# First attention: group outputs taken inside the next Q/K normalisation; local layers: first K and Q at the end of the FFN

## The chip, the cores and the metric

The kernel runs on one core of a Trainium2 chip. The metric is the time of one execution on the device in microseconds (us), the median of several. The core has a matrix engine (TensorE, PE in the profile; PEld is its weight load), three others that compute (VectorE = DVE, ScalarE = ACT, GpSimd = POOL) and SyncE (SP), which here issues all DMAs. Each engine runs its own program in order; they wait for each other at semaphores.

## The reference, cut to what matters

`x` has 8 batches of 512 rows of 128 values, all in float32. Two blocks are added to it in turn:

```python
xn = layernorm(x)
x = x + attn0(xn) + ffn0(xn)   # attn0: differential causal attention, 16 q/k heads of 8, 8 value heads of 16
                               #   q, k: rms-normalised, rotated; y = y1 - lambda * y2, then Wproj
                               # ffn0: one linear layer on inputs quantised in blocks of 32
xn = layernorm(x)
x = x + attn1(xn) + local(xn)  # attn1: plain attention, 16 heads of 8
def local(x):                  # 6 layers, 16 heads of 64, window 32
    for i in range(6):
        x = attn_layer(shift_tokens(x), ...) + x
        x = ffn_layer(shift_tokens(x), ...) + x
```

`shift_tokens` takes the upper half of the columns from the row before. `attn_layer` forms q, k, v with one weight of 128 x 3072, l2-normalises and rotates q and k, attends within windows of 32 rows and the window before, and multiplies by Wo. `ffn_layer` is a layer norm, a gated product and a product back to 128 columns.

## The kernel before, in words

The program has four phases, one behind another with a barrier between: the first attention with its linear layer (up to about 400 us), the second attention (to about 895 us), the six local layers (to about 4403 us), and the sum and the output.

**First attention.** All engines walk through one list `steps` of triples (b, j, k): batch b, group j of four heads (four groups to a batch), head k. Group number t = 4b + j. In step (b, j, k) TensorE makes the scores of head k of group t and, from k = 1 on, the products with the values of group t - 1; ScalarE takes the exponentials. At k = 0 ScalarE copies the sums of group t - 2 to `OT` (L448), at k = 1 TensorE transposes them (L369) and VectorE divides them into `Y` (`outputs`, L520 to L528). The other work is laid between these steps and shares one PSUM bank (7), which each user may take only after the reader of the last user is done (`claim`):
- `in_prep(b)`, batches -2 to 5: batch b + 2 is prepared. Transposes of its normalised rows `XL` (L363) at (0, 0), Q/K/V products (L377) at (0, 2), (0, 3), (1, 0), (1, 2), VectorE's copies of them (L630, L631), ScalarE's squares (L490) and VectorE's `normal` (L508 to L513) at (1, 3): a reduction, eleven short operations of which ten are the root (`rsqrt`, L111 to L115), and a multiplication in place (L513). Then GpSimd rotates queries and keys (`rotated`, L695 to L698, twice), TensorE transposes them at (3, 0) and (3, 2) (L424), VectorE copies them to `QR` and `KR` (L648), GpSimd splits them into three bfloat16 parts (`parts`, L706 and L709), and SyncE writes these to DRAM and packs the groups from there. For batch 1 the transposes stand at (0, 0, 0) and (0, 0, 1).
- `done(b)`, batches 1 to 8: the outputs of batch b - 1. Transposes of `Y` (L396) at (1, 3), of the quantised rows `xd` (L402) at (2, 0), the projection (L412, L413) at (2, 3); VectorE adds the bias (`pr`, L636) and adds the result to the rows `X1` (L639).
- VectorE's quantising of batch b is a generator of 17 operations (`quant_steps`, L195 to L211), of which it runs one at the end of each step of the batch (`next(work)`) and the rest at (3, 3).
- Before step (0, 0, 0) VectorE runs the rest of its list `early`, which ends with the normalisation of the rows of batches 2 to 7 (`scaled(2, B)`, L571) and the quantising of the weight.

**Local layers.** Each engine has a loop over the six layers. A layer's attention goes over 32 row tiles of 128 (`tiles`), three tiles in flight: in a slot the front tile gets K, V, Q products (L1383, L1393 or L1454, L1448; the first tile has its own order, 1), ScalarE squares and copies them, VectorE multiplies by cosines and sines (L1667, L1672) and sums the squares, GpSimd takes the root and scales (L1286 to L1308); the middle tile is transposed (L1424, L1467), the last one attends. SyncE copies the values into windows, 20 DMAs a tile. The FFN (`layer`, run through `ahead`) takes the batches in pairs; at its end TensorE transposes the rows of batch 0 (`rows_up`, L1331) for the next layer. ScalarE copies them to `xsT` (L1524, L1525) at the head of its next turn of the layer loop, and TensorE's first K product stands at the head of its own next turn, behind the waits for these rows and for the weights. The weights of layer l's attention are loaded by SyncE at the head of its turn l, once the attention of layer l - 1 is done.

## Time and profile before

| | us |
|---|---|
| median of 3 runs (lowest, highest) | 4410.02 (4403.59, 4414.05) |
| the profiled execution: its time | 4421.74 |
| its span, first to last instruction | 4419.9 |
| TensorE busy | 4084.9 (92%) |
| VectorE busy | 3323.8 (75%) |
| GpSimd busy | 2596.7 (59%) |
| ScalarE busy | 2372.8 (54%) |

The mean granted TensorE clock was 0.976 of full speed. A row of the view in order of time has: start, duration, engine, line, operation, output and inputs, how many instructions are merged into it, and in brackets the engine's idle time before it and what ended it. VectorE's next instruction can start some 0.08 us before the end shown for the last.

### The profile page before, as it was taken

The numbers are of one execution on the slowest core, as the hardware profiler recorded it, in microseconds if no ns is written. First come the engines' busy times: TensorE is split into PE (matmuls) and PEld (weight loads), VectorE is DVE, ScalarE is ACT, GpSimd is POOL, SyncE is SP. The second block draws the span as 40 slices with busy tenths as digits, with TensorE's granted clock in tenths as the row PEclk, the third lists the DMA queues.
The fourth block names the chain that finished last, engine by engine and source line by source line (L and its number), as shares of the span: only waits on it lengthen the run. The fifth ranks groups of instructions, "written<-read, shape, count | busy, mean of one in ns | idle before, by whom it ended". The sixth has DMA issues, their size and how long they took to land. (4 is left out here: it accounts for less than half of the span.)

```text
span 4419.9 us, 164515 instructions
## 1 busy us (share of the span) xinstructions
PE 4084.9 (92%) x68421; PEld 2658.5 (60%) x68421; DVE 3323.8 (75%) x5603; ACT 2372.8 (54%) x3396; POOL 2596.7 (59%) x3647
## 2 busy tenths in 40 slices
PE   4888999979998899988999989999899998899997
PEld 2554333357676576765777666777557676577765
DVE  7785988768876678776787767878668886688775
ACT  3654777745554455544555544555445554455543
POOL 5452111077774477762878727777357875377770
PEclk9998999989999999999999999999999999999999
DMA  2222111033332133221332303323123232133320
GB/s 76 86 79 65 54 56 53 28 87 81 79 80 56 48 80 80 75 61 46 78 82 76 78 25 82 84 73 83 42 58 83 77 81 64 38 79 79 81 68 20
DMA packets 216797, 298.60 MB, mean 68 GB/s; under 512 B 44241, under 2 KB 110801, under 8 KB 215377
## 3 DMA queue, kind: packets, MB, share of 16 engines
q1 hardware_dynamic: 216144, 288.46, 24.3%
q8 instruction: 585, 9.58, 0.9%
q14 instruction: 68, 0.55, 0.0%
HBM read 58.13 MB, written 14.68 MB: 16 GB/s over the span
## 5 line engine op out<-in xcount | busy, mean ns | idle before, releaser
L1542 ACT ACTIVATE ls_r<-PS 128x1024 f32<-128x1024 f32 x192 | 196.6, 1024 | 782.8 <-PE PS L1383 782.8
L1677 DVE TENSOR_REDUCE ls_ss<-ls_r 128x16 f32<-128x1024 f32 x384 | 465.7, 1214 | 99.1 <-ACT ls_r L1579 99.1
L1667 DVE TENSOR_TENSOR ls_a<-PS,TC 128x1024 f32<-128x1024 f32 x384 | 467.5, 1219 | 94.1 <-ACT ls_r L1542 90.8
L1286 POOL TENSOR_TENSOR ls_a<-ls_a,ls_q 128x1024 f32<-128x1024 f32 x192 | 453.9, 2364 | 99.0 <-DVE ls_q L1672 99.0
L1672 DVE TENSOR_TENSOR ls_q<-PS,TS 128x512 f32<-128x512 f32 x768 | 491.3, 681 | 0.0
L1306 POOL TENSOR_TENSOR ls_a<-ls_a,ls_q 128x1024 f32<-128x1024 f32 x192 | 456.7, 2379 | 0.0
L1448 PE MATMUL PS<-WQ,ls_xsT 128*128 128x512 f32 x768 | 398.8, 642 | 4.0 <-issue 4.0
L1579 ACT ACTIVATE ls_r<-PS 128x1024 f32<-128x1024 f32 x186 | 190.7, 1026 | 392.7 <-PE PS L1448 392.7
L1474 PE MATMUL PS<-WO,ls_r 128*128 128x128 f32 x3072 | 398.6, 284 | 0.5 <-ACT ls_r L1583 0.5
L1383 PE MATMUL PS<-WQ,ls_xsT 128*128 128x512 f32 x768 | 382.5, 621 | 16.3 <-issue 9.9
L1308 POOL TENSOR_TENSOR ls_a<-ls_a,ls_rn 128x1024 f32<-128x1024 f32 x192 | 365.6, 1904 | 15.1
L1303 POOL TENSOR_TENSOR ls_a<-ls_a,ls_rn 128x1024 f32<-128x1024 f32 x192 | 365.4, 1903 | 15.0
L1474 PEld LDWEIGHTS PS<-WO,ls_r 128*128 128x128 f32 x3072 | 363.2, 194 | 18.1 <-ACT ls_r L1583 1.9
L1393 PE MATMUL PS<-WQ,ls_xsT 128*128 128x512 f32 x744 | 349.6, 592 | 0.0
L1019 DVE TENSOR_REDUCE mxs<-PS 128x2 f32<-128x1024 f32 x256 | 305.9, 1220 | 50.9 <-PE PS L873 48.6
L954 ACT ACTIVATE PT<-PS 128x512 f32<-128x512 f32 x512 | 282.0, 599 | 109.0 <-PE PS L882 102.8
L1704 DVE RECIPROCAL ls_rc<-PS 128x14 f32<-128x14 f32 x192 | 47.2, 246 | 372.3 <-PE PS L1438 372.2
L1317 POOL TENSOR_TENSOR ls_r<-XL,B 128x512 f32<-128x512 f32 x48 | 61.1, 1294 | 452.5 <-DVE XL L1751 326.3
L1438 PE MATMUL PS<-ls_vb,ls_q 64*32 64x65 f32 x24576 | 289.6, 228 | 40.0 <-issue 29.8
L1368 PE MATMUL PS<-ls_kT,ls_qT 64*32 64x64 f32 x24576 | 317.4, 225 | 0.0
L1684 DVE TENSOR_REDUCE ls_mx<-PS 128x8 f32<-128x512 f32 x384 | 263.3, 686 | 70.8 <-PE PS L1368 66.6
L1368 PEld LDWEIGHTS PS<-ls_kT,ls_qT 64*32 64x32 f32 x24576 | 279.8, 105 | 50.0 <-issue 43.5
(274 smaller groups left out, 8653.9 us busy)
## 6 DMA issues: line engine op xcount, KB each, us to landing
ls_vb<-ls_vt SPq DMA_DIRECT2D x1152, 130.0 KB
ls_vb<-ls_vt SPq DMA_DIRECT2D x672, 65.0 KB
QT<-scratch SPq DMA_DIRECT2D x576, 32.0 KB
KT<-scratch SPq DMA_DIRECT2D x576, 32.0 KB
ls_xs<-XL SPq DMA_DIRECT2D x42, 256.0 KB, 3.3
WQ<-wqkv SPq DMA_DIRECT2D x6, 1536.0 KB, 6.5
ls_vb<-ls_vz SPq DMA_DIRECT2D x96, 65.0 KB
scratch<-QP SPq DMA_DIRECT2D x48, 128.0 KB, 1.8
```

What stands on the lines that cost most here:

```text
L1286: pool.tensor_tensor(a4[:, 1], a4[:, 1], b4[:, 1], ALU.add).then_inc(s_ck, 1)
L1303: pool.tensor_tensor(a4[:, 1], a4[:, 1], scale(1), ALU.mult).then_inc(s_nk, 1)
L1306: pool.tensor_tensor(a4[:, 0], a4[:, 0], b4[:, 0], ALU.add).then_inc(s_cq, 1)
L1308: pool.tensor_tensor(a4[:, 0], a4[:, 0], scale(0), ALU.mult).then_inc(s_nq, 1)
L1368: ins = pe.matmul(banks(S_BANK[a])[WIN * w:WIN * w + WIN, i * 2 * WIN:(i + 1) * 2 * WIN], qT[r, i, WIN * w:WIN * w + WIN], kT[r, i, k0:k0 ...
L1383: ins = pe.matmul(banks(K_BANK + c), rows, WQ[:, INNER + c * 512:INNER + c * 512 + 512], start=True, stop=True)
L1393: ins = pe.matmul(banks((V_BANK if order > 2 else V_EARLY) + e), rows, wv[:, e], start=True, stop=True)
L1448: ins = pe.matmul(banks(Q_BANK + c), rows, WQ[:, c * 512:c * 512 + 512], start=True, stop=True)
L1474: ins = pe.matmul(banks(W_BANK)[:, 0:D], YT[:, i * P:i * P + P], WO[:, i, :], start=(i == 0), stop=(i == INNER // P - 1))
L1667: nc.vector.tensor_tensor(v4(A[fq])[:, a], src, tab, ALU.mult).then_inc(done, 1)
L1672: ins = nc.vector.tensor_tensor(v4(SW)[:, a, :, lo:lo + h2], src[:, :, hi:hi + h2], TS[:, ft, a, lo:lo + h2].unsqueeze(1).to_broadcast([P, ...
L1677: nc.vector.tensor_reduce(ss[:, fq, a * H:a * H + H], v4(SQ)[:, a], AX.X, ALU.add).then_inc(done, 1)
```

## The change

In the first attention:
- each of the multiplications that normalise the rows counts up `s_ln`, and TensorE's transposes of batch n wait for n + 1;
- for batches 0 to 5 the outputs of the batch's first group (t - 1 at j = 1) are taken at (1, 3) inside `normal`, after the fourth operation of `rsqrt`, and no longer at (2, 1);
- the addition to `X1` moves from (2, 3) to (3, 0), behind VectorE's copy of the queries;
- at (2, 0) and (2, 3) VectorE runs no quantising step; (3, 3) runs what is left.

In the local layers:
- TensorE makes K and Q of the next layer's first tile (`first_tile`) behind the last FFN product, before the layer loop turns, and once ahead of the loop; V stays in the loop;
- ScalarE copies the rows for it (`staged`) at the end of its turn;
- after the last layer this is done once more for nothing, with weights that SyncE loads again for it.

```diff
@@ first attention, TensorE
                         if in_prep(b) and (j, k) == (0, 0):
                             claim(s_xe, n + 1)
-                            pe.wait_ge(s_ln, min(n, 2) + 1)
+                            pe.wait_ge(s_ln, n + 1)
@@ first attention, VectorE
-                    def normal(n):
+                    def normal(n, between=None):
...
-                        rsqrt(link, rms[:, 1, :, :], rms[:, 0, :, :], rms[:, 2, :, :])
+                        done = [0]
+
+                        def linked(ins):
+                            link(ins)
+                            done[0] += 1
+                            if between is not None and done[0] == 4:
+                                outputs(between)
+
+                        rsqrt(linked, rms[:, 1, :, :], rms[:, 0, :, :], rms[:, 2, :, :])
...
-                            ins = dve.tensor_tensor(o, o, wide(sums[:, 2, i, :]), ALU.mult)
-                            if i < 2 or i == hi - 1:
-                                ins.then_inc(s_ln, 1)
+                            dve.tensor_tensor(o, o, wide(sums[:, 2, i, :]), ALU.mult).then_inc(s_ln, 1)
...
-                        if k == 1 and 0 <= t - 2 < GROUPS:
+                        if k == 1 and 0 <= t - 2 < GROUPS and not (j == 2 and in_prep(b)):
                             outputs(t - 2)
...
                         if in_prep(b) and (j, k) == (1, 3):
-                            normal(n)
+                            normal(n, t - 1 if 0 <= t - 1 < GROUPS else None)
...
-                            dve.wait_ge(s_wb, b)
-                            dve.tensor_tensor(X1[:, (b - 1) * NT:b * NT, :], X1[:, (b - 1) * NT:b * NT, :], pr[:, :, :], ALU.add).then_inc(s_x1, 1)
...
+                        if done(b) and (j, k) == (3, 0):
+                            dve.wait_ge(s_wb, b)
+                            dve.tensor_tensor(X1[:, (b - 1) * NT:b * NT, :], X1[:, (b - 1) * NT:b * NT, :], pr[:, :, :], ALU.add).then_inc(s_x1, 1)
...
                         if 0 <= b < B:
-                            next(work, None)
+                            if (j, k) not in ((2, 0), (2, 3)):
+                                next(work, None)
@@ local layers, SyncE: the loads of the attention weights are now attn_weights(l, opened)
+                attn_weights(DEPTH - 1, DEPTH + 1)
+                sp.wait_ge(w_attn, DEPTH * 96 + 96)
@@ local layers, TensorE
+                def first_tile(l):
+                    pe.wait_ge(s_xe, l * B + 1)
+                    pe.wait_ge(w_attn, l * 96 + 96)
+                    pe.wait_ge(s_xl[0], (l + 1) * PAIRS)
+                    rows = xsT[0][:, XO - 1:XO - 1 + P]
+                    for at, col, done in ((K_BANK, INNER, s_k), (Q_BANK, 0, s_q)):
+                        for c in range(2):
+                            ins = pe.matmul(banks(at + c), rows, WQ[:, col + c * 512:col + c * 512 + 512], start=True, stop=True)
+                        ins.then_inc(done, 1)
...
+                first_tile(0)
                 with loop(pe, 0, DEPTH) as l:
...
-                        if front:
+                        if front and order > 1:
...
+                        if not more:
+                            first_tile(l + 1)
@@ local layers, ScalarE
+                def staged(l, b):
+                    act.wait_ge(s_xt, l * B + b + 1)
+                    act.activation(xsT[0][0:DH, XO - 1:XO - 1 + T], banks(X_BANK)[0:DH], ACT.Copy)
+                    act.activation(xsT[0][DH:P, XO:XO + T], banks(X_BANK)[DH:P], ACT.Copy).then_inc(s_xe, 1)
+
+                staged(0, 0)
...
-                    tiles(act, lambda: prep(0), slot, lambda b: None, prep)
+                    tiles(act, lambda: None, slot, lambda b: None, prep)
...
                         if more:
                             ready(p + 1)
+                        else:
+                            staged(l + 1, 0)
```

## Rows read from the trace of the kernel before

**Rows 1.** The page: busy time of TensorE, share of the span, instructions.
```profile
PE 4084.9 (92%) x68421; PEld 2658.5 (60%) x68421; DVE 3323.8 (75%) x5603; ACT 2372.8 (54%) x3396; POOL 2596.7 (59%) x3647
```

**Rows 2.** Waits up to 420 us: who for whom, us in total, times, longest.
```profile
PE PS L412 <- DVE Y L525: 10.9, 5, 2.2
...
PE PS L369 <- DVE QR L648: 4.2, 5, 1.6
```

**Rows 3.** VectorE in order of time, batch 5 and into 6.
```profile
297.17 1.23 DVE L513 TENSOR_TENSOR qk<-qk,rms 128x1024 f32<-128x1024 f32 x1
...
299.79 0.26 DVE L520 RECIPROCAL rec<-PS 128x16 f32<-128x16 f32 x1
...
302.16 1.37 DVE L205 TENSOR_SCALAR qa<-qa 128x512 f32<-128x512 f32 x1
...
306.71 0.69 DVE L648 COPY QR<-PS 128x512 f32<-128x512 f32 x1
...
316.31 0.26 DVE L520 RECIPROCAL rec<-PS 128x16 f32<-128x16 f32 x1
```

**Rows 4.** TensorE in order of time: first Q/K/V product in batch 4.
```profile
238.72 0.91 PE L377 MATMUL PS<-W,xT 128*128 128x384 f32 x2 [0.37 <-DVE Y L528]
```

**Rows 5.** TensorE's waits in the local layers.
```profile
PE PS L1383 <- issue: 9.9, 6, 2.3
```

**Rows 6.** TensorE in order of time, seam of the first two local layers.
```profile
1482.24 2.84 PE L1511 MATMUL PS<-WB,ls_a 128*128 128x128 f32 x24
1486.93 1.98 PE L1383 MATMUL PS<-WQ,ls_xsT 128*128 128x512 f32 x4 [1.85 <-issue]
...
1490.46 1.88 PE L1454 MATMUL PS<-WQ,ls_xsT 128*128 128x512 f32 x4
```

**Rows 7.** TensorE and VectorE in order of time, start of batch 0.
```profile
70.12 1.08 PE L363 MATMUL PS<-CT,XL 128*128 128x128 f32 x4 [5.38 <-DVE XL L571]
...
77.23 0.69 DVE L648 COPY QR<-PS 128x512 f32<-128x512 f32 x1
```

**Rows 8.** VectorE in order of time, normalisation in batch 0.
```profile
95.80 0.29 DVE L115 SCALAR_TENSOR_TENSOR rms<-rms 128x128 f32<-128x128 f32 x1
...
98.09 1.23 DVE L513 TENSOR_TENSOR qk<-qk,rms 128x1024 f32<-128x1024 f32 x1
...
104.24 0.26 DVE L520 RECIPROCAL rec<-PS 128x16 f32<-128x16 f32 x1 [3.56 <-PE PS L369]
```

**Rows 9.** TensorE in order of time, the same stretch.
```profile
103.05 1.08 PE L369 MATMUL PS<-CT,OT 128*128 128x128 f32 x4
...
108.27 0.60 PE L424 MATMUL PS<-CT,qk 128*128 128x128 f32 x4
```

**Rows 10.** TensorE in order of time, batch 5.
```profile
300.65 0.46 PE L412 MATMUL PS<-WFT,xdT 128*128 128x128 f32 x2 [2.18 <-DVE Y L525]
...
304.52 1.02 PE L424 MATMUL PS<-CT,qk 128*128 128x128 f32 x4
```

**Rows 11.** GpSimd in order of time, batch 5: end of the queries' rotation.
```profile
301.66 1.59 POOL L698 TENSOR_TENSOR qk<-qk,sq 128x512 f32<-128x512 f32 x1
```

**Rows 12.** VectorE in order of time, batch 3 and into 4.
```profile
216.99 1.23 DVE L513 TENSOR_TENSOR qk<-qk,rms 128x1024 f32<-128x1024 f32 x1
...
237.12 0.26 DVE L520 RECIPROCAL rec<-PS 128x16 f32<-128x16 f32 x1
```

**Rows 13.** VectorE in order of time, batch 6, GpSimd idle.
```profile
335.71 0.43 DVE L205 TENSOR_SCALAR qa<-qa 128x512 f32<-128x512 f32 x1
```

**Rows 14.** ScalarE in order of time, second tile of the second local layer.
```profile
1501.62 1.03 ACT L1571 ACTIVATE ls_vt<-PS 128x1024 f32<-128x1024 f32 x1 [6.04 <-DMA ls_vb<-ls_vt]
1503.48 1.02 ACT L1575 ACTIVATE ls_kT<-PS 128x1024 f32<-128x1024 f32 x1 [0.83 <-PE PS L1424]
```

**Rows 15.** TensorE and VectorE in order of time, end of the program.
```profile
4399.61 2.84 PE L1511 MATMUL PS<-WB,ls_a 128*128 128x128 f32 x24
...
4409.66 4.91 DVE L1767 TENSOR_TENSOR X<-X,XL 128x512 f32<-128x512 f32 x8 [6.39 <-PEq L131]
```

More of the change, by code:

```diff
@@ L1208, in _, with attn_weights @@
             def _(sp):
-                with loop(sp, 0, DEPTH) as l:
-                    sp.wait_ge(free_attn, l + 1)
+                def attn_weights(l, opened):
+                    sp.wait_ge(free_attn, opened)
                     sp.dma_start(WQ[:, :], wqkv[l]).then_inc(w_attn, 16)
@@ L1215, in _ @@
                     sp.dma_start(QK[:, :, :], qkscale[l].rearrange("p (a e) -> p a e", a=2)).then_inc(w_attn, 16)
+                with loop(sp, 0, DEPTH) as l:
+                    attn_weights(l, l + 1)
                     sp.wait_ge(free_ffn, l + 1)
@@ L1344, in begin @@
                     def begin():
-                        pe.wait_ge(s_xl[0], (l + 1) * PAIRS)
+                        pass
                     def lead(front, back, order):
@@ L1372, in lead @@
                                         ins.then_inc(s_so, 1)
-                        if front:
+                        if front and order > 1:
                             if ft == 0:
                                 pe.wait_ge(s_xe, l * B + fb + 1)
-                                pe.wait_ge(w_attn, l * 96 + 96)
                             if order == 3:
@@ L1446, in slot @@
                                 pe.wait_ge(s_ve, nf)
-                            for c in range(2):
-                                ins = pe.matmul(banks(Q_BANK + c), rows, WQ[:, c * 512:c * 512 + 512], start=True, stop=True)
-                            ins.then_inc(s_q, 1)
+                                for c in range(2):
+                                    ins = pe.matmul(banks(Q_BANK + c), rows, WQ[:, c * 512:c * 512 + 512], start=True, stop=True)
+                                ins.then_inc(s_q, 1)
                             if order == 1:
```

## The prediction

> **What bounds the kernel now.** I read the page's busy times first: TensorE is busy 92% of the span [rows 1], so most time can only come back where it waits. Then I read each engine in order of time in the three stretches that the change touches: the first attention (up to about 400 us), the seam between two of the six local layers, and the end of the program.
>
> In the first attention there are eight batches of four groups. In batches 0 to 5 VectorE also normalises the queries and keys of the batch two further on. Read in order of time, one such batch shows a tight loop of three engines. TensorE waits 2.2 us ahead of the output projection in five batches, for group outputs that VectorE took late [rows 2]. But VectorE has next to nothing to spare: from the last multiplication of the normalisation to the outputs of the group in step (0, 1) of the next batch it works almost without a break, 297.17 to 316.31 [rows 3]. TensorE's next Q/K/V product, in step (0, 2), then waits for exactly those outputs, 0.37 us in the batch shown [rows 4]. So at the end of each batch VectorE decides, not TensorE.
>
> At the seam of two local layers TensorE has a gap of 1.85 us ahead of the first K product, with no wait behind it [rows 6]; it comes six times, 9.9 us together [rows 5]. That is the back edge of the layer loop.
>
> **The change part by part**
>
> **1. A count per batch of normalised rows.** The transposes of batch 2 waited to 70.12, 5.38 us of it in idleness, for the last of six multiplications [rows 7]; now the first suffices. But the next user of that bank after the queries' transposes is the keys' transposes, and these need VectorE's copy of the queries at 77.23 [rows 7]. VectorE reaches that copy only after all of its early list, which is unchanged. Worth 0 (bounds -1 to 0 us).
>
> **2. Outputs inside the normalisation, batch 0.** The new place, after the fourth step of the root, is passed at 95.80 + 0.29 = 96.1; the outputs need the transposes of group 0, which end at 103.05 + 1.08, so VectorE now stands until 104.24 [rows 8, 9]. Before, it finished the normalisation in that time. Behind the wait stand the outputs (0.73 us), six steps of (98.09 - 95.80) / 7 = 0.327 us, and the last multiplication of 1.23: done at 108.16 instead of 99.32, 8.8 us later. GpSimd's rotation starts on it, and its first half takes some 4.6 us (4.8 in batch 5, from 298.4 to 301.66 + 1.59 [rows 3, 11]): done at about 112.8. TensorE's transposes of the queries, at 108.27 before [rows 9], wait for it: 4.5 us late, and everything in order behind them. Part 3's order adds up to 1.5 us in the same batch. I take 6 us (4.5 to 7.5: the upper end if TensorE, after the stall, runs for some us at the lower clock, as its four transposes of 1.08 us at 103.05 do, behind a stall, against 0.60 for four at 108.27).
>
> **3. The same in batches 1 to 5, with the new order behind it.** Here the transposes are done in time, and the outputs cost the normalisation only their own 0.75 us and a short wait: about 0.87 us. The projection no longer waits: 300.65 becomes about 298.5 [rows 10], a gain of 2.2 us at that point. What is late next is the rotation. Its first half ends at 301.66 + 1.59 = 303.25 [rows 11]; 0.87 later, less what GpSimd gains by fewer collisions, is 304.0. So the queries' transposes run at 304.05 instead of 304.52: of 2.2 us, 0.5 is left. VectorE's copy of the queries comes at 304.75 instead of 306.71, but VectorE is idle for some 2 us before it, since two quantising steps and the residual addition have been put behind. Its work is the same: from 298.31 (right behind the last multiplication) to 316.31 are 18.0 us, less the outputs' 0.75 is 17.25. Of that, 3.8 us lie before the copy (two quantising steps to 299.79, 1.48; one from 300.54 to 302.16, 1.62; the bias addition, about the copy's 0.69), 13.4 from it on. 304.75 + 13.4 = 318.15 against 316.31: 1.8 us later. In batches 3 and 4 the same stretch takes 19.0 us (218.1 to 237.12 [rows 12]), 1 us more, in which VectorE waits for a slower projection; the new order takes up such waits, so the loss there is 1 us less, 0.8. Sum 3 x 1.8 + 2 x 0.8 = 7 us later. Bounds: 5 x 1.8 = 9; or VectorE makes up for it and TensorE's own gain of about 1 us in each batch counts, -5.
> The durations in this sum hold collisions: the same quantising step takes 1.37 us at 302.16, while GpSimd's addition of 301.66 to 303.25 runs, and 0.43 at 335.71 with GpSimd idle [rows 3, 11, 13].
> The Trainium skill (SBUF — State Buffer, "SBUF: two separate sides") says that VectorE operations with two SBUF inputs or in a fast mode and GpSimd's hold a port pair in turn, each for its whole length. This trace agrees (1.37 against 0.43 us). The rule speaks against the new order: GpSimd has no pause from the rotation to the keys' parts, so each of the nine such operations behind the copy waits for one of GpSimd's. Stepped through by that rule a batch like 5 comes out 1.85 us later, and batches 3 and 4 some 1.0, not 0.8: 7.5 us for the part in place of 7.
> In batches 6 and 7 there is no normalisation, VectorE has idle time, and the moved steps are hidden.
>
> **4. First K and Q at the end of the FFN.** At five seams K follows the last FFN product directly: the gap of 1.85 (9.9 / 6 on average, 9.7 at the five, as the first layer has none) goes from the path K, squares, VectorE, GpSimd, first K transposes. Behind the Q product the back edge still stands, now ahead of V. V's own path has little to spare: the second V copy at 1501.62 and its 1.03 us end at 1502.65, and the K copy behind it begins at 1503.48 [rows 14]. If V came a full 1.9 us behind Q, the two would not move together, and only some 0.5 us per seam would be left. But eight products of 0.44 us (1486.93 to 1490.46) now lie ahead of the back edge, against 24 of 0.12 us (2.84 / 24 [rows 6]), so the sequencer has time to run ahead. I take 1.8 us per seam, 9 in all (bounds 2.5 to 9.7). The squares on ScalarE and the cosines on VectorE stand behind their own back edges, which they reach before the product is done.
> The Trainium skill (TensorE: Matmul & The Clock Gate, the table of the specifications) gives TensorE a queue of 64 instructions. By that the back edge would vanish wholly behind the eight products and the seam gives its 9.7 us; no row here shows the queue itself.
> In layer 0 the K product waits for a DMA anyway, and the loop's entry now stands between Q and V; of at most 1.9 us V's path can hide 0.8: an estimate of +0.3 us (0 to 1.1).
>
> **5. The end.** Before, TensorE's last product begins at 4399.61 and lasts 2.84 us, and VectorE's final additions start at 4409.66 behind the barrier [rows 15]. Now eight more products stand behind it, 8 x 0.44 = 3.5 us, of which VectorE's last addition (it starts when the product ends and takes about 0.7) hides 0.7: +2.8 us (0 if the barrier doesn't wait for them, 3.6 at most). The extra weights load during the last FFN, where nothing else loads.
>
> **Sum**: 0 + 6 + 7 + 0.3 - 9 + 2.8 = +7.1 us. The profiled execution took 4421.7 us (span 4419.9), 11.7 over the median of 4410.0; I add the sum to the median: 4417 us.
>
> **The rivals**
> - *The V product pays the back edge (slower).* If the gap before V is over about 1 us, the V copies and window loads decide the first slots, and a seam gives 0.5 us: 6 + 7 + 0.3 - 2.5 + 2.8 = +13.6, 4424. For it: V's path has only 0.8 us to spare. Against: the long products ahead.
> - *The late keys of batch 2 (slower).* The 8.8 us of part 2 delay the keys' parts, their write and the packing of group 6; if that lands after batch 1 asks for it, the stall grows by 3 to 5 us: about +11, 4421. Against: TensorE is 6 us late there itself.
> - *VectorE's steps fall between GpSimd's (no change).* Then TensorE's own gain of 1 us per batch counts: 4.5 - 5 + 0.3 - 9 + 2.8 = -6.4, 4403.6.
> - *The change does what it seems to be for (faster).* The waits ahead of the projection (10.9 us in five batches) and behind the queries' copy (4.2 in five [rows 2]) both go, and GpSimd's rotation is no wait: 4.5 - 15.1 + 0.3 - 9 + 2.8 = -16.5, 4393.5. Against it: rows 3 and 11, where neither VectorE nor GpSimd has that time.
>
> **How the numbers follow.** What a measurement of this kernel tells from no change is about 0.2%, 8.8 us. The forecast has 50% (own range +2 to +13; three parts in ten of it over +8.8), the V rival 17%, the late keys 7%, the fallen-between case 13%, the full gain 13%. Slower: 15 + 17 + 7 = 39, so 40%; the same: 35 + 13 = 48, less a little for unknowns, 46%; faster 14%. The range is 4402 to 4426: it holds the forecast, most of both slower cases and the -6.4 case, and leaves out the full gain.
>
> **What would show it.** In batch 0 VectorE idle from 96.1 to 104.2 inside the root, and the queries' transposes at about 112.7. In batches 1 to 5 no wait ahead of the projection, a wait of 1.5 to 2 us ahead of the queries' transposes on the rotation, VectorE idle about 2 us before the copy, and a longer wait for the outputs ahead of the Q/K/V product of (0, 2). The first attention 12 to 14 us longer. At the seams K right behind the last FFN product, V without a gap, the first K transposes 1.8 us earlier. At the end the barrier about 3 us later. The forecast is wrong if the first attention doesn't get longer, or if a seam gives under 1 us.

## The result and the profile after

The changed kernel takes 4428.42 us (median of 20 runs, 4411.17 to 4438.18) against 4412.36 for the kernel before (20 runs, 4403.59 to 4419.63): ratio 1.0034, 95% interval 1.0027 to 1.0042, so 12 to 19 us slower. The forecast had the direction and less than half of the size: 4417, +7.1, with a range up to 4426. Of all executions in this document one stands apart, one of 11960 us in the experiment e2, whose cause was not seen; its ratio is taken without it. The profiled execution of the changed kernel took 4420.04 us (span 4418.2), 8 us under its median, while the one of before took 4421.74, 9 us over its own. So the two spans alone say nothing of the change; the traces must be compared stretch by stretch, and the experiments must give the prices.

The totals are the same as in [rows 1]: TensorE's busy time is equal within 0.3 us. That is a balance of two things: it is busy 8.7 us longer in the first attention, and shorter in the second attention and in the layers.

```profile
PE 4084.6 (92%) x68429; PEld 2655.4 (60%) x68429; DVE 3317.9 (75%) x5603; ACT 2374.9 (54%) x3398; POOL 2597.4 (59%) x3647
```

By stretches (view by windows: start:end, its length, busy us of each engine with instructions, granted clock as a share of full speed, DMA share, GB/s; the engines in the order PE, PEld, DVE, ACT, POOL) the first attention ends 22.1 us later in the changed kernel: the first product of the second attention is at 425.82 instead of 403.75. The second attention, which no edit touches, takes 2.3 us less, with TensorE busy 3.3 us less for the same products, so the local layers start 19.7 us later (917.91 against 898.17). A local layer is shorter. Before, the first attention from 83 us on, the second attention, and the second local layer:

```profile
83.00:403.75 320.75, 274.13 (x2471) 162.46 (x2470) 226.81 (x464) 186.60 (x188) 147.90 (x147) 0.94 0.26 80
403.75:898.17 494.42, 453.37 (x2513) 159.81 (x2513) 406.44 (x569) 351.87 (x645) 76.93 (x103) 0.96 0.17 52
...
2065.60:2649.50 583.90, 555.15 (x10562) 387.23 (x10561) 436.20 (x735) 301.25 (x423) 388.17 (x558) 0.98 0.27 69
```

The same stretches of the changed kernel:

```profile
83.00:425.82 342.82, 282.86 (x2472) 162.00 (x2470) 221.98 (x464) 186.93 (x188) 148.30 (x147) 0.92 0.24 75
425.82:917.91 492.09, 450.10 (x2512) 158.74 (x2513) 406.83 (x569) 350.59 (x644) 76.93 (x103) 0.97 0.17 52
...
2075.30:2655.50 580.20, 552.82 (x10562) 386.34 (x10561) 436.05 (x735) 301.28 (x423) 388.12 (x558) 0.98 0.27 69
```

**Batch 0.** VectorE in order of time, against [rows 8], then TensorE, against [rows 9]. VectorE stands inside the root for 8.04 us, the last multiplication is at 106.46 instead of 98.09, and the queries' transposes start at 112.59 instead of 108.27:

```profile
95.42 0.29 DVE L115 SCALAR_TENSOR_TENSOR rms<-rms 128x128 f32<-128x128 f32 x1
103.75 0.26 DVE L528 RECIPROCAL rec<-PS 128x16 f32<-128x16 f32 x1 [8.04 <-PE PS L369]
...
106.46 1.23 DVE L521 TENSOR_TENSOR qk<-qk,rms 128x1024 f32<-128x1024 f32 x1
```

```profile
112.59 1.12 PE L424 MATMUL PS<-CT,qk 128*128 128x128 f32 x4 [4.66 <-POOL qk L706]
```

The next normalisation starts at 141.18 instead of 134.10: up to there batch 0 costs 7.1 us.

**Batches 1 to 5.** The waits of TensorE up to 430 us, against [rows 2]. The 10.9 us ahead of the projection are gone. In their place stand the rotation (22.3 us in seven, 4.66 of them in batch 0) and the outputs of step (0, 1), for which the Q/K/V product waits 12.6 us in five places, up to 2.9:

```profile
PE PS L424 <- POOL qk L706: 22.3, 7, 4.7
...
PE PS L377 <- DVE Y L536: 12.6, 5, 2.9
```

The wait for the outputs of (0, 1) in the kernel before:

```profile
PE PS L377 <- DVE Y L528: 2.4, 5, 0.7
```

VectorE in order of time, batch 5 and into 6, answers to [rows 3]. Read the time from each row to the next, and the idle times in brackets: from the last multiplication (317.82) to the queries' copy 6.83 us, from the copy to the outputs of (0, 1) 14.30, with a wait of 1.29 on TensorE in it:

```profile
317.82 1.23 DVE L521 TENSOR_TENSOR qk<-qk,rms 128x1024 f32<-128x1024 f32 x1
...
324.65 0.69 DVE L652 COPY QR<-PS 128x512 f32<-128x512 f32 x1 [2.48 <-PE PS L424]
325.26 0.68 DVE L655 TENSOR_TENSOR X<-X,pr 128x512 f32<-128x512 f32 x1
325.86 1.49 DVE L205 TENSOR_SCALAR qa<-qa 128x512 f32<-128x512 f32 x1
328.64 0.26 DVE L528 RECIPROCAL rec<-PS 128x16 f32<-128x16 f32 x1 [1.29 <-PE PS L369]
...
334.73 1.54 DVE L210 TENSOR_TENSOR qa<-qa,qb 128x512 f32<-128x512 f32 x1
336.30 0.98 DVE L211 TENSOR_TENSOR xd<-qa,qs 128x512 f32<-128x512 f32 x1
...
338.95 0.26 DVE L528 RECIPROCAL rec<-PS 128x16 f32<-128x16 f32 x1
```

From one normalisation to the next the four periods from batch 1 on are 41.93, 43.41, 41.94 and 43.44 us, against 39.08, 39.09, 40.08 and 40.10 before: 12.4 us in four batches. Of these 12.4 us TensorE is busy 5.0 longer (145.06 against 140.04 in the four periods) and idle 7.4 longer. By windows, the first two of them, changed kernel. The longer of the two has more of the lower clock in it (0.92 of full speed against 0.96) and 1.55 us more of busy TensorE for the same products, so the step from 41.9 to 43.4 goes with the clock:

```profile
141.18:183.11 41.93, 35.49 (x317) 20.43 (x316) 31.46 (x66) 23.89 (x25) 21.95 (x21) 0.96 0.26 79
183.11:226.52 43.41, 37.04 (x318) 20.93 (x316) 32.24 (x66) 24.01 (x25) 21.94 (x21) 0.92 0.25 76
```

**The seam** of the first two local layers, the engines in order of time, against [rows 6]. K and Q follow the last FFN product without a gap, V follows Q without a gap, and the next idle time of TensorE is for VectorE's sines (1.78 us). VectorE itself comes to the first cosines 3.56 us after its last instruction of the old layer, with nothing to wait for but its own way round the loop (in the view, "issue": idle time with no wait that the profile shows). ScalarE's squares of K are done at 1502.79 + 1.02 = 1503.81, 1.6 us before these cosines start:

```profile
1498.19 2.84 PE L1534 MATMUL PS<-WB,ls_a 128*128 128x128 f32 x24
...
1500.87 3.60 PE L1354 MATMUL PS<-WQ,ls_xsT 128*128 128x512 f32 x8
...
1501.78 0.06 DVE L1788 MEMSET ls_mx<- 128x1 f32 x1
...
1502.79 1.02 ACT L1573 ACTIVATE ls_r<-PS 128x1024 f32<-128x1024 f32 x1 [1.90 <-PE PS L1354]
...
1504.31 1.88 PE L1477 MATMUL PS<-WQ,ls_xsT 128*128 128x512 f32 x4
...
1505.40 1.23 DVE L1700 TENSOR_TENSOR ls_a<-PS,TC 128x1024 f32<-128x1024 f32 x1 [3.56 <-issue]
...
1507.97 1.96 PE L1406 MATMUL PS<-WQ,ls_xsT 128*128 128x512 f32 x4 [1.78 <-DVE ls_q L1705]
```

**The end**, against [rows 15]: the barrier comes 2.6 us later behind VectorE's last addition (9.00 against 6.39).

```profile
4408.00 4.91 DVE L1800 TENSOR_TENSOR X<-X,XL 128x512 f32<-128x512 f32 x8 [9.00 <-PEq L131]
```

### The profile page after: what moved, and what is told of

It reads as the page before. It is cut to its first block and busy times, and to the rows that moved or that the text cites. A ratio compares the mean times of both kernels' runs of the same rounds, so it can differ in the third digit from the quotient of the medians.

```text
span 4418.2 us, 164505 instructions
## 1 busy us (share of the span) xinstructions
PE 4084.6 (92%) x68429; PEld 2655.4 (60%) x68429; DVE 3317.9 (75%) x5603; ACT 2374.9 (54%) x3398; POOL 2597.4 (59%) x3647
## 5 line engine op out<-in xcount | busy, mean ns | idle before, releaser
L1471 PE MATMUL PS<-WQ,ls_xsT 128*128 128x512 f32 x744 | 380.6, 635 | 0.1
L1406 PE MATMUL PS<-WQ,ls_xsT 128*128 128x512 f32 x744 | 368.3, 617 | 9.4 <-DVE ls_q L1705 9.3
L1416 PE MATMUL PS<-WQ,ls_xsT 128*128 128x512 f32 x744 | 350.6, 593 | 0.0
```

Source lines behind the costliest of these rows:

```text
L1406: ins = pe.matmul(banks(K_BANK + c), rows, WQ[:, INNER + c * 512:INNER + c * 512 + 512], start=True, stop=True)
L1416: ins = pe.matmul(banks((V_BANK if order > 2 else V_EARLY) + e), rows, wv[:, e], start=True, stop=True)
L1471: ins = pe.matmul(banks(Q_BANK + c), rows, WQ[:, c * 512:c * 512 + 512], start=True, stop=True)
```

## The experiments

The theory after the first comparison: the first attention is the whole loss, and in it the new order of VectorE's steps, because they pile up ahead of the outputs of step (0, 1). The rivals: the outputs inside the normalisation cost by themselves; TensorE's lower clock behind the new waits is the cost; the local layers lose in most runs. Each time below has the kernel before beside it, on the same chip; its median there is 4416.83 (first four), 4413.82 (next four) and 4417.73 (last four). The ratio with its interval is not that of the two medians (in e8 it differs from it by 0.0017), and the verdicts go by the interval. "Layers start" is when the first local layer begins, 898.17 in the kernel before; the expectations speak of it. It holds the second attention too, which no edit touches and which takes 491.5 us in some traces and 494.4 in others. So each trace is also read at the end of the first attention, which is the first product of the second one: 403.75 before. A period is the time from one normalisation's start to the next.

**e1_attention_alone.** All edits of the first attention, none of the local layers.

> The kernel before with the edits of the first attention alone (outputs inside the normalisation, residual addition behind the queries' copy, the two skipped quantising steps, the count per batch). In the changed kernel's profile the first local layer starts 19.7 us later than before (917.91 against 898.17). Theory (the first attention is the whole loss, the layers give next to nothing): +18 to +21 us, ratio about 1.0045; the profile shows 43.4 and 41.9 us in turn from one multiplication of the normalisation to the next. Rival (the layers' edits lose too, and the attention's 19.7 hold a part that comes from elsewhere): +8 to +14. First forecast's terms: +13.

4442.36 us, ratio 1.0066 (1.0053 to 1.0079). The layers start at 919.42, +21.2; the first attention ends at 426.21, +22.5. The periods are 41.57, 43.24, 42.09 and 43.67. So the first attention is the whole loss; the trace gives the expected size, the runs 23 to 35 us, more than either theory.

**e2_layers_alone.** The edits of the local layers alone:

```diff
+                        if not more:
+                            first_tile(l + 1)      # K and Q, behind the last FFN product
...
+                        else:
+                            staged(l + 1, 0)       # ScalarE's first copies of the rows
```

> The kernel before with the edits of the local layers alone (first K and Q at the end of the FFN, first copies of the rows there, weights loaded once more at the end). Theory (at each seam VectorE's own loop entry, 3.6 us, takes the place of TensorE's gap; 0.5 us is left per seam, and the end costs 2.6): 5 x -0.5 + 0.3 + 2.6 = 0, within -3 to +3 us. Rival 1 (the six layers really are 24 us shorter, as in the changed kernel's profile): -24 + 2.6 = about -21. Rival 2 (the layers lose in most runs, and the profiled one was lucky): +3 or more. First forecast's terms: -9 + 0.3 + 2.8 = -6.

4408.28 us, ratio 0.9980 (0.9971 to 0.9989), so 5 to 13 us faster. Neither rival, and the theory's 0 is outside too; the first forecast's -6 for these parts is inside. 1.0066 x 0.9980 is 1.0046: the two halves add up to the whole change, 1.0027 to 1.0042, within their intervals.

**e3_outputs_alone.** Only the outputs inside the normalisation:

```diff
+                            if between is not None and done[0] == 4:
+                                outputs(between)
...
-                        if k == 1 and 0 <= t - 2 < GROUPS:
+                        if k == 1 and 0 <= t - 2 < GROUPS and not (j == 2 and in_prep(b)):
```

> Of the first attention's edits only the group outputs taken inside the normalisation; the residual addition and the quantising steps stay where they were. Theory (the new order of VectorE costs what the outputs' place doesn't: about 7 us in batch 0, the rest in batches 1 to 5 by the order): +7 to +10 us, the projection without a wait ahead of it, and the period of batches 1 to 5 near 39.1. Rival (the early outputs cost by themselves, since VectorE now waits for the transposes): +14 to +20, the period near 41.9 as in the changed kernel.

4423.27 us, ratio 1.0016 (1.0003 to 1.0028); layers start +9.7, first attention +12.0. The time and the layers' start have the theory's size; the first attention by itself lies between theory and rival, and so do the periods, 40.02, 41.82, 40.04 and 41.82. In these four TensorE is busy 6.9 us longer than before (146.90 against 140.04) and idle 1.5 us less: what e3 loses there goes with the lower clock. Its waits from 140 to 305 us show the rotation in full and the outputs of (0, 1) hardly:

```profile
PE PS L424 <- POOL qk L706: 12.0, 4, 3.0
PE PS L377 <- DVE Y L536: 2.6, 2, 1.3
```

**e4_attention_but_batch0.** All of the attention's edits, the outputs of batch 0 where they were:

```diff
-                            normal(n, t - 1 if 0 <= t - 1 < GROUPS else None)
+                            normal(n, t - 1 if b >= 1 and t - 1 < GROUPS else None)
```

> The first attention's edits, but in batch 0 the outputs stay behind the normalisation. All theories that take batch 0 from the trace: 7.1 us less than the first attention's edits in full, so about +12.6 us over the kernel before. Rival (the stall of batch 0 is made good later, so it costs nothing in the end): the same time as with all of the first attention's edits, +18 to +21.

4432.76 us, ratio 1.0036 (1.0023 to 1.0049); layers start at 913.07, 6.35 us sooner than with all of the edits (919.42), and the first attention ends at 420.92, 5.3 us sooner (+17.2). Most of batch 0's cost stays lost: the rival falls. The whole is +14.9 in the trace, not 12.6, because all of the attention's edits were 21.2 and not 19.7 there.

**e5_outputs_and_residual and e6_outputs_and_skips.** The outputs inside the normalisation with one of the two changes of order each:

```diff
+                        if done(b) and (j, k) == (3, 0):       # e5: the addition to X1, behind the copy
...
+                            if (j, k) not in ((2, 0), (2, 3)):  # e6
                                 next(work, None)
```

> Outputs inside the normalisation and the residual addition behind the queries' copy; the quantising steps stay. In the profile of the outputs alone VectorE stands 2.26 us ahead of the outputs of step (3, 1), waiting for TensorE, so 0.7 us put ahead of that wait cost nothing. Theory (waits have room there): the same as the outputs alone, local layers start 9 to 11 us later than before, time +6 to +10. Rival (each microsecond put behind the copy is paid, as the forecast's part 3 summed it): 6 x 0.7 = 4 us more than the outputs alone.

> Outputs inside the normalisation and the two quantising steps skipped (they then come later in the batch); the residual addition stays. In the changed kernel the TensorE product of step (0, 2) waits 2.9 us for the outputs of (0, 1), and runs at the lower clock after it; in the kernel with the outputs alone this wait is 0 to 1.3. Theory (the skipped steps push the outputs of (0, 1) back, and the wait that this makes is what the changed kernel pays beyond the outputs alone): local layers start 17 to 21 us later than before, wait of 2 to 3 us ahead of the product of (0, 2) in each of batches 1 to 5. Rival (the skips are covered by VectorE's 2.26 us wait in step (3, 1)): as the outputs alone, +9 to +11.

e5: 4425.60, ratio 1.0017 (1.0006 to 1.0028), layers start +8.3, first attention +9.7: the residual addition costs nothing. e6: 4440.05, ratio 1.0047 (1.0031 to 1.0062), layers start +22.2, 1.2 us over the theory's range, first attention +23.3: the two skipped steps are the whole difference between the outputs alone and all of the attention's edits. TensorE's waits from 140 to 305 us, e5 and then e6:

```profile
PE PS L424 <- POOL qk L707: 12.0, 4, 3.0
PE PS L377 <- DVE Y L536: 3.0, 3, 1.1
```

```profile
PE PS L424 <- POOL qk L707: 13.0, 4, 3.3
PE PS L377 <- DVE Y L536: 10.2, 4, 2.7
```

The wait for the rotation is nearly the same; the wait for the outputs of (0, 1) is what the skips add.

**e7_order_alone.** Residual addition moved and steps skipped, the outputs where they were.

> The residual addition and the skipped quantising steps without the outputs inside the normalisation. Theory (VectorE's order alone): TensorE reaches the projection about 0.7 us and the queries' transposes earlier, since the outputs of (2, 1) stand one quantising step further forward; the outputs of (0, 1) come no earlier, since VectorE's work is the same. Within -4 to +4 us of before. Rival (the order costs by itself, 1.2 to 1.8 us per batch, whatever the outputs do): +7 to +11.

4422.03 us, ratio 1.0007 (0.9996 to 1.0019); layers start at 899.64, +1.5, but the first attention ends at 408.01, +4.3: the unchanged second attention is 2.8 us shorter in this trace. The time can't tell theory from rival; the trace lies just over the theory's +4. The same skips that cost 11.3 us beside the early outputs (e6 less e3) cost 4.3 or less without them. The waits from 140 to 305 us say why:

```profile
PE PS L377 <- DVE Y L528: 10.3, 4, 2.6
PE PS L412 <- DVE Y L525: 7.1, 5, 1.4
PE PS L424 <- POOL qk L700: 2.4, 4, 0.6
```

The pile ahead of (0, 1) is there as well (10.3 us), 8.1 us more than the 2.2 before, but the projection waits 3.8 us less than the 10.9 before, the waits behind the queries' copy are gone (4.0 of the 4.2 us in [rows 2] lie here), and the rotation costs only 2.4: what TensorE loses at one wait it mostly gains at two others. With the outputs inside, the rotation's 12 us and the pile's 10 both stand.

**e8_only_k_moved.** As e2, with K alone at the end of the FFN:

```diff
-                    for at, col, done in ((K_BANK, INNER, s_k), (Q_BANK, 0, s_q)):
+                    for at, col, done in ((K_BANK, INNER, s_k),):
```

> The local layers' edits with K alone at the end of the FFN; the first Q product stays at the start of the layer. Theory (the seam is now bound by VectorE's own loop entry, 3.55 us from its last addition to the first cosines, which waits for K's squares alone): the layers as with both moved, 3.5 to 4 us shorter each than before, and the end 1.8 us cheaper since only four of eight products stand there: -10 to -13 us against before. Rival 1 (Q ahead of the back edge is what brings the gain): half the gain or less, -5 to 0. Rival 2 (with four long products instead of eight ahead of it, TensorE's back edge shows again, 1 to 1.9 us, ahead of Q and V, and V's path decides): K transposes no earlier than before, -2 to +3.

4406.38 us, ratio 0.9966 (0.9954 to 0.9979), 9 to 20 us faster: the theory's size, and both rivals are outside. At a seam (2061.15, in order of time) the back edge shows again for 1.27 us behind only four products, and yet the K product of the next tile waits only 0.24 us, and the first K transposes come 18.64 us after the start of the last FFN product, as in the changed kernel (18.75):

```profile
2061.15 2.84 PE L1526 MATMUL PS<-WB,ls_a 128*128 128x128 f32 x24
2063.83 1.88 PE L1346 MATMUL PS<-WQ,ls_xsT 128*128 128x512 f32 x4
2066.99 1.96 PE L1463 MATMUL PS<-WQ,ls_xsT 128*128 128x512 f32 x4 [1.27 <-issue]
...
2068.33 1.23 DVE L1692 TENSOR_TENSOR ls_a<-PS,TC 128x1024 f32<-128x1024 f32 x1 [3.53 <-issue]
...
2070.89 1.95 PE L1398 MATMUL PS<-WQ,ls_xsT 128*128 128x512 f32 x4 [0.24 <-DVE ls_q L1697]
...
2079.79 1.97 PE L1439 MATMUL PS<-CT,ls_a 128*128 128x128 f32 x8 [5.22 <-POOL ls_a L1308]
```

The Q and V products come some 1.4 us later than in the changed kernel and the transposes 0.1 us sooner, so their place doesn't set the first transposes. VectorE's loop entry does, as far as the traces show: 3.53 us at this seam, and the first cosines again 1.6 us behind the end of K's squares (2066.77). The barrier at the end comes 7.29 us behind VectorE's last addition, 0.9 over before in place of 2.6: two thirds of the end's cost are gone.

**e9_changed_with_steps_ahead and e10_before_with_steps_ahead.** Two quantising steps taken early, in the changed kernel and in the kernel before:

```diff
+                            if (j, k) in ((0, 2), (0, 3)):
+                                next(work, None)
```

> The changed kernel with two quantising steps of each batch taken early, one more in step (0, 2) and one more in (0, 3), where VectorE stands 1.6 us before the copies behind the Q/K/V product. The two skipped steps then no longer pile up ahead of the outputs of (0, 1). Theory (the pile ahead of those outputs, not the skipping, is what costs): the wait ahead of the product of (0, 2) falls from 2.9 us to under 1, local layers start 17.7 us - 12 = 6 to 10 us later than before instead of 19.7, and the time is 4408 to 4418 on a chip where before is 4412. Rival (the product was late because of the rotation and the clock, the outputs only came last): waits move elsewhere, local layers start 16 us or more later than before.

> The kernel before with the same two quantising steps taken early and nothing else. Theory (VectorE's stretch from the normalisation to the outputs of (0, 1) sets the period of a batch, 39.1 to 40.1 us): that stretch loses 1.5 to 3 us, but TensorE's own wait there is only 0.4 to 0.7 per batch, so 0.5 to 1 us per batch comes back: -2 to -6 us. Rival (the steps ahead delay the next normalisation, whose start waits 0.95 us for ScalarE): 0 to +5.

e9: 4414.73 us, ratio 0.9998 (0.9988 to 1.0007); layers start at 902.74, +4.6 in place of +19.7, and the first attention ends at 411.24, +7.5 in place of +22.1. These two lines take back 14.6 us, two thirds of the first attention's loss, and 13.7 of them are idle time of TensorE. With the layers' gain the kernel is level with before. Its waits from 140 to 305 us:

```profile
PE PS L424 <- POOL qk L708: 10.6, 4, 2.7
PE PS L377 <- DVE Y L536: 3.2, 3, 1.3
```

e10: 4418.72, ratio 1.0002 (0.9992 to 1.0012); layers start at 895.36, 2.8 us sooner, and the first attention ends 2.6 us sooner. The trace has the theory's size; the runs can't tell it from no change.

TensorE's clock doesn't explain what the two lines gave back, but it isn't excluded for the rest. In four periods TensorE is busy 144.54 us in e9 and 145.06 in the changed kernel, nearly the same, and yet e9's four periods are 10.1 us shorter:

```profile
141.22:301.87 160.65, 144.54 (x1266) 83.46 (x1264) 125.73 (x264) 95.57 (x97) 86.21 (x84) 0.94 0.26 79
```

```profile
141.18:311.90 170.72, 145.06 (x1265) 82.70 (x1264) 127.46 (x265) 95.81 (x97) 87.88 (x84) 0.94 0.25 76
```

Against before (158.35, busy 140.04) e9's periods are 2.3 us longer, with TensorE busy 4.5 us longer and idle 2.2 us less. Over the whole first attention it is 7.5 us longer and busy 7.7 longer. Either idle time takes up part of the lower clock, or the clock eats what the shorter waits gave; no run separates the two.

**e11_before_k_moved_steps_ahead and e12_same_with_outputs_inside.** e8, with the count per batch and the steps ahead; and the same with the outputs inside the normalisation in batches 1 to 5.

> The kernel before with K alone moved to the end of the FFN, the count per batch of normalised rows, and the two quantising steps taken early. If the parts add up: the -12 to -15 us of K alone plus the steps ahead, -14 to -20 us. If the steps ahead cost: -10 or less gain.

> The previous kernel with the group outputs inside the normalisation in batches 1 to 5 as well (not in batch 0, and without the changes of VectorE's order). Theory (TensorE's wait moves from the projection to the rotation and nothing is gained): within -3 to +5 us of the previous kernel, with a wait of 2.5 to 3 us ahead of the queries' transposes. Rival (with the outputs of (0, 1) relieved, the 2.2 us ahead of the projection come back): 4 to 10 us under the previous kernel.

e11: 4401.10 us, ratio 0.9966 (0.9954 to 0.9978), layers start at 893.09, 5.1 us sooner than before. It beats both kernels, 10 to 20 us under before; K alone has the same ratio, so nothing that the times can tell comes from the steps ahead. e12: 4406.86 us, ratio 0.9976 (0.9967 to 0.9985), layers start at 898.61, 5.5 us later than in e11, just over the theory's +5; the rival is refuted. Even with batch 0 spared and no pile, the outputs inside the normalisation don't pay. The wait ahead of the rotation, from 140 to 305 us, takes the place of the others: TensorE's waits sum to 17.9 us in e11 and to 18.0 in e12. The 5.5 us themselves go with the clock, since TensorE is busy 6.6 us longer in e12's first attention for the same products.

```profile
PE PS L424 <- POOL qk L706: 13.6, 5, 2.7
```

**All traces together.** The first attention against before, in us: how much longer it is, how much longer TensorE is busy in it (from 60 us on), and how much longer it is idle. e2 and e8 have none of its edits and show how far two traces of the same code differ.

| kernel | longer | busy | idle |
|---|---|---|---|
| changed | +22.1 | +8.5 | +13.5 |
| e1, attention alone | +22.5 | +10.1 | +12.4 |
| e6, outputs and skips | +23.3 | +10.9 | +12.4 |
| e4, all but batch 0 | +17.2 | +9.9 | +7.2 |
| e3, outputs alone | +12.0 | +10.0 | +2.1 |
| e5, outputs and residual | +9.7 | +5.4 | +4.3 |
| e9, changed, steps ahead | +7.5 | +7.7 | -0.2 |
| e7, order alone | +4.3 | +1.1 | +3.2 |
| e12, outputs in batches 1 to 5, steps ahead | +0.6 | +4.8 | -4.2 |
| e10, before, steps ahead | -2.6 | +2.1 | -4.8 |
| e11, count, steps ahead | -4.9 | -1.8 | -3.1 |
| e2 and e8, no edit here | +0.4, +0.2 | +1.5, +1.5 | -1.1, -1.3 |

The skips beside the early outputs bring idle time (e6 against e3: +10.3 of 11.3), which e9 takes back. The early outputs themselves bring busy time, that is lower clock (e3: 10.0 of 12.0; e12 against e11: 6.6 of 5.5). That the lower clock is the cause of their loss is not shown; it is a rival to the wait for the rotation, and no run holds one of them fixed.

## Why the prediction was wrong in size

- **Part 1**, worth 0: as forecast. The transposes of batch 2 no longer wait, but the first normalisation of batch 0 starts only 0.4 us sooner (92.99 against 93.38), less than the traces with the same code there differ (92.6 to 93.9).
- **Part 2**, +6 (4.5 to 7.5): right in its steps. 8.04 us of waiting, the transposes at 112.59 (forecast 112.7), 7.1 us up to the next normalisation, and 5.3 us at the end of the first attention (e4 against e1).
- **Part 3**, +7: this step failed, in its size. The mechanism was right: no wait ahead of the projection, the rotation late next, VectorE deciding at (0, 1). The forecast made the outputs of (0, 1) 1.85 us late in batch 5. Measured from the start of its normalisation they are at 338.95 - 311.90 = 27.05 us against 316.31 - 292.45 = 23.86: 3.2 us late. The terms: the normalisation with the outputs takes 5.92 instead of 4.72 (1.2, where 0.87 was taken); to the copy 6.83 (6.71 forecast); and "13.4 from it on" measured 14.3. That figure moved 13.4 us of work behind the copy and took VectorE to be busy throughout, but the same new order makes VectorE meet TensorE too early, and it stands 1.29 us ahead of the outputs of (3, 1). VectorE's total work was a lower bound of that stretch, and was used as its length. Over all: 12.4 us in the periods of batches 1 to 4 and 2.6 from there to the end of the first attention, 15.0 for the 7 forecast. The bound of 5 x 1.8 = 9 was too low by the same mistake, and by a second one: part 3 has no term for TensorE's clock, which part 2 had thought of. TensorE is busy 5.0 us longer in the four periods, and the longer periods of the changed kernel are the ones with more of the lower clock. How much of the 12.4 us this is can't be said: of e9's 4.5 us of longer busy time at most 2.3 show in its periods, unless its shorter waits had gained something by themselves.
- **What the forecast saw in the order and what not.** It priced the skips and the residual addition together. e5 and e6 part them: nothing (2.4 us less than the outputs alone) and 11.3 us. The two skipped steps don't vanish; they run in one piece behind (3, 3), where the row of outputs of (0, 1) waits behind them.
- **Part 4**, -9: the gap went, V had none, as forecast. But it missed that VectorE's own back edge, 3.56 us, is late next: "which they reach before the product is done" is refuted, and at the second seam the first K transposes come 2094.01 - 2075.26 = 18.75 us behind the start of the last FFN product, against 2085.02 - 2065.63 = 19.39 before: 0.6 us earlier and not 1.8, under the 1 us that the forecast itself named as a sign of being wrong. Yet a layer as a whole is shorter by more than that: 583.1 us on average over the last five layers of the eight traces without the layers' edits, 580.4 over the six with them: 2.8 us per seam, 14 in all. Part of it is clock: TensorE's busy time in these layers is 554.4 us on average in the first group and 553.3 in the second, for the same products. Where in the layer the rest comes from is not settled; no run was made for it. The expectation of e2 (0.5 us per seam) was wrong by trusting the first transposes alone. The second seam before, and in the changed kernel:

```profile
2065.63 2.84 PE L1511 MATMUL PS<-WB,ls_a 128*128 128x128 f32 x24
...
2085.02 1.97 PE L1424 MATMUL PS<-CT,ls_a 128*128 128x128 f32 x8 [5.25 <-POOL ls_a L1303]
```

```profile
2075.26 2.84 PE L1534 MATMUL PS<-WB,ls_a 128*128 128x128 f32 x24
...
2094.01 1.33 PE L1447 MATMUL PS<-CT,ls_a 128*128 128x128 f32 x5 [5.24 <-POOL ls_a L1316]
```

- **Layer 0**, +0.3: wrong in sign, 582.1 against 583.9 on average over the same traces, -1.8. **Part 5**, +2.8: measured 2.6, and 0.9 with K alone.

The terms read from traces are 7.1 + 15.0 for the first attention, -2.3 for the second, -14 - 1.8 for the layers and +2.6 for the end: +6.6, next to the forecast's +7.1, but by chance. Two errors, 9 us too little loss in parts 2 and 3 and 7 us too little gain in the layers, nearly cancel, and the rest is the second attention's different clock in two traces, which no part of the change explains.

And the timed result is +16. For what is left, some 9 us, there is only the clock of each run to go by. The six runs of the changed kernel with a mean granted clock of 0.974 take 4427.9 us on average, the four with 0.976, one of them the profiled run, 4420.6. With the lower level at half speed, 0.002 of the mean are 0.004 of 4420 us spent there, 17.7 us, of which half, 8.8, is lost if nothing hides it. Run e1 has the same sign (0.973, and +23 to +35 timed against +21.2 in its trace). So the changed kernel's trace is one with more clock than its usual run. That fits, but in which stretch the usual runs lose it was not seen, and the clocks of the 20 runs of the kernel before are not on record. The layers' part may hold some of it too: the traces give -14 - 1.8 + 2.6 = -13.2 for the layers' edits, and e2's times 5 to 13 us.

The rivals: "the V product pays" is refuted (no gap at V). "The late keys of batch 2" didn't come: the whole stall of batch 0 is 7.1. "VectorE's steps fall between GpSimd's" and "the change does what it seems to be for" are refuted by the result, and e3 and e12 show where: without waits ahead of the projection nothing comes back.

## What to carry to other kernels

A work item that is skipped in a slot is moved, not saved: find the slot where it runs instead, and what stands behind it there. Here two skipped steps of 1 us landed ahead of the one group of outputs that TensorE waits for; two lines that took them earlier, into slots where VectorE had idle time, gave 14.6 of the first attention's 22.1 us back. When a stretch of an engine is lengthened or shortened in a sum, its busy time is only its floor: ask which of the other engines it will meet too early. And when a back edge is taken from one engine's path, look for the back edges of the others at the same place: VectorE's 3.56 us stood where TensorE's 1.85 had gone. And when a stage is timed by the start of a later one, make sure that what lies between took the same time: here the untouched second attention differed by up to 2.9 us between traces, and made e7's 4.3 us look like 1.5.

## What the runs showed of the hardware

- Of the way round the outer loop 3.56 us show on VectorE with nothing to wait for, and 1.85 on TensorE before [rows 6]. Behind eight long products (3.60 us) TensorE's doesn't show at all, behind four (1.88 us) it shows 1.27 us. So TensorE's sequencer seems to have run ahead of its products. The Trainium skill (TensorE: Matmul & The Clock Gate, the table of the specifications) states a queue of 64 instructions for the engine; with eight the trace agrees, and with four it shows that depth alone doesn't hide the edge, the products must also last.
- TensorE's granted clock falls to its lower level, half speed, behind most of the waits of 2 to 3 us, but not behind all. In the changed kernel's four periods six of eight waits of 2.88 to 2.95 us are followed by 3 to 4 us at 0.50, and those of 169.48 and 254.84 are not; before, three of four waits of 2.2 us are. In the changed kernel the wait of 2.93 us for the rotation ends at 152.89, and four windows show the granted clock (the number ahead of the last two): 1.00 ahead of the wait, 0.50 from 155 to 157, 1.00 from 158 on, and 0.50 again from 213 to 215, behind the 2.88 us that the product of (0, 2) waited. The products of four batches took 140.04 us of TensorE before and 145.06 in the changed kernel. What that costs in time differs: the changed kernel's periods with two such stretches are 1.5 us longer than those with one, while before a period with one takes 39.09 us and a period with none 39.08.

```profile
147.00:152.00 5.00, 2.96 (x32) 2.45 (x24) 3.98 (x5) 2.40 (x3) 3.65 (x4) 1.00 0.28 85
155.00:157.00 2.00, 2.00 (x12) 0.85 (x5) 1.28 (x1) 0.60 (x1) 1.92 (x2) 0.50 0.11 31
158.00:161.00 3.00, 3.00 (x41) 1.77 (x38) 1.68 (x4) 1.72 (x2) 2.78 (x4) 1.00 0.02 5
213.00:215.00 2.00, 2.00 (x21) 0.96 (x19) 0.12 (x1) 1.24 (x1) 0.00 (x0) 0.50 0.32 95
```
